# Gate and up of a feed-forward block made in parts of 512, 512 and 384 columns instead of four of 352, with new orders in the second pass

## What is computed

```
xn = layernorm(x)
Q, K, V = elu(xn@Wq+bq)+1, elu(xn@Wk+bk)+1, xn@Wv+bv          # 16 heads of 64
KV = einsum('bshd,bhdm->bhdm', K, V);  Z = 1/(Q . sum(K) + eps)
a  = einsum('bshd,bhdm,bsh->bshm', Q, KV, Z) @ Wo + bo
x1 = layernorm(xn + a)*g1 + be1
s  = layernorm(x1 + gelu(x1@W1+b1)@W2 + b2)*g2 + be2
xq = fp4(xn)                                                   # blocks of 16, also the weights
h  = silu(xq @ wg.T) * (xq @ wu.T)                             # 704 wide
g  = silu(fp4(h) @ wd.T)
out = x + s*g
```

## Time and profile before

| what | value |
|---|---|
| median of 3 runs | 1630.44 us (1628.6 to 1631.35) |
| the profiled execution | 1627.72 us |
| its span (first to last instruction) | 1625.9 us |
| PE busy | 1598.0 us, 98% |
| DVE busy | 1277.0 us, 79% |
| ACT busy | 977.1 us, 60% |
| POOL busy | 788.5 us, 48% |
| DMA | 123.96 MB, 76 GB/s on average |
| granted TensorE clock | 0.999 over the span |

### The profile page before, as it was taken

The page is one execution under the profiler, slowest core; times in us unless marked ns, Lnnn a source line. Parts: engine busy times, 40 slices in busy tenths (PEclk is TensorE's granted clock), DMA queues, the critical chain, the costliest instruction groups (busy, mean ns, idle before and its releaser), DMA issues.

```text
span 1625.9 us, 30464 instructions
## 1 busy us (share of the span) xinstructions
PE 1598.0 (98%) x10977; PEld 1439.4 (89%) x10977; DVE 1277.0 (79%) x2487; ACT 977.1 (60%) x1770; POOL 788.5 (48%) x750
## 2 busy tenths in 40 slices
PE   8999999999999999999999999999999999999997
PEld 6878888888889998989999999989899999999897
DVE  6786665545688797978888887979788888879797
ACT  6665665656465747465665657474755656574743
POOL 4564544434242636455544546364555445463636
PEclk9999999999999999999999999999999999999999
DMA  7422322331511111122121112111111221111110
GB/s 226 137 88 85 107 68 102 106 116 65 168 36 55 53 54 53 55 108 59 68 86 55 53 54 107 55 53 54 53 58 65 100 99 54 55 53 55 53 54 27
DMA packets 90531, 123.96 MB, mean 76 GB/s; under 512 B 10496, under 2 KB 58764, under 8 KB 89359
## 3 DMA queue, kind: packets, MB, share of 16 engines
q1 hardware_dynamic: 90382, 122.03, 23.0%
HBM read 86.86 MB, written 35.14 MB: 75 GB/s over the span
## 4 chain that ended last, share of the span: by engine, by line
PE 83%; DVE 9%; issue 3%; ACT 3%; POOL 2%; DMA 0%; DVEq 0%; SPq 0%; POOLq 0%; ACTq 0%
PE QH L81 11%; PE QH L82 11%; PE QH L83 11%; PE AC L81 7%; PE AC L83 7%; PE AC L82 7%; PE GU L81 5%; PE GU L83 5%; PE GU L82 5%; PE TT L834 2%; PE DN L726 2%; PE DN L81 2%; PE DN L82 2%; PE DN L83 2%; DVE rl L1846 1%
## 5 line engine op out<-in xcount | busy, mean ns | idle before, releaser
L2321 POOL TENSOR_TENSOR hb<-hb,rs_h 128x704 f32<-128x704 f32 x64 | 89.1, 1392 | 206.3 <-DVE rs_h L1689 206.3
L1253 ACT ACTIVATE hb<-GU 128x352 f32<-128x352 f32 x128 | 59.2, 463 | 214.7 <-PE GU L83 214.7
L1206 ACT ACTIVATE rh<-QH 128x512 fp32r<-128x512 f32 x256 | 150.4, 599 | 39.0 <-DVE QH L1837 35.4
L81 PE MATMUL GU<-wgh,xqh 128*128 128x352 f32 x512 | 169.5, 331 | 2.9 <-DVE hb L1682 2.9
L83 PE MATMUL GU<-wgh,xql 128*128 128x352 f32 x512 | 165.1, 322 | 0.0
L82 PE MATMUL GU<-wgl,xqh 128*128 128x352 f32 x512 | 164.9, 322 | 0.0
L2327 POOL TENSOR_TENSOR hb<-hb,sn_h 128x64 f32<-128x64 f32 x64 | 18.8, 293 | 296.9 <-DVE hb L1694 296.9
L1852 DVE TENSOR_TENSOR rl<-QH,rh 128x512 fp32r<-128x512 f32 x128 | 86.0, 682 | 85.6 <-ACT rh L1206 83.5
L81 PE MATMUL AC<-w2h,rh 128*128 128x256 f32 x512 | 145.8, 285 | 0.0
L81 PE MATMUL AC<-Mh,rh 128*128 128x256 f32 x512 | 145.3, 284 | 0.1
L82 PE MATMUL AC<-w2l,rh 128*128 128x256 f32 x512 | 142.4, 278 | 0.0
(11 more groups left out here) (235 smaller groups left out, 5589.3 us busy)
## 6 DMA issues: line engine op xcount, KB each, us to landing
zb<-z_scratch SPq DMA_DIRECT2D x128, 256.0 KB, 3.5
xa<-in_L_attn_src SPq DMA_DIRECT2D x16, 512.0 KB, 4.2
xt_scratch<-xth SPq DMA_DIRECT2D x32, 256.0 KB, 2.6
xt_scratch<-xtl SPq DMA_DIRECT2D x32, 256.0 KB, 3.0
xb<-in_L_attn_src SPq DMA_DIRECT2D x16, 512.0 KB, 4.0
xnTh<-xt_scratch SPq DMA_DIRECT2D x32, 256.0 KB, 4.8
xnTl<-xt_scratch SPq DMA_DIRECT2D x32, 256.0 KB, 5.5
out<-x SPq DMA_DIRECT2D x15, 512.0 KB, 6.6
```

What stands on the lines that cost most here:

```text
L81: e.matmul(outp, lh, rh, start=start, stop=False, skip_group_check=check)
L1206: e.activation(RH[j % 4][:], src, ACT.Copy).then_inc(S[sem], 1)
L1253: e.activation(HB[i % 3][:, hf * HALF:(hf + 1) * HALF], gu_bank(i, hf)[:, 0:HALF], ACT.Tanh, scale=0.5).then_inc(S["th"], 1)
L2321: e.tensor_tensor(hb, hb, spread(rs_h[i % 2][:], 44), ALU.mult).then_inc(S["hin"], 1)
```

## The change

The weights lie in other sections: 512 gate, 512 up, 192 gate, 192 up. `gate_up(i, 0)` makes 512 gate columns into the first bank and 512 up columns into the second, with a signal after each; `gate_up(i, 1)` makes 192 gate and 192 up in one product of 384 columns in one bank, the first for even tiles and the second for odd, with one signal. A tile has 12 matmuls of 512 and 6 of 384 columns. The waits are for the part that is overwritten alone: `hu` where only the gate columns of the bank must have been read, `hh` where up columns. `gate_tanh` and `gate_mul` work on 512 and 192 columns. The code that loads the weights follows the sections, and a few unused columns of SBUF are put between tensors. The bank choice "QH" for gate_up, unused before, is gone. Lines shift by one to some eighty (mm3 is L80 to L82 then).

```diff
-HALF = 352
+HEAD = 512
+SECTIONS = ((0, 512, 0, 0), (512, 512, 1, 0), (1024, 192, 0, 512), (1216, 192, 1, 512))
-GU_ORDER = (((0, 1), "GU"), ((0, 0), "GU"), ((1, 0), "GU"), ((1, 1), "GU"), ((2, 1), "GU"), ((2, 0), "GU"), ((3, 0), "GU"), ((3, 1), "GU"))
+GU_ORDER = ((0, 0), (0, 1), (1, 1), (1, 0), (2, 0), (2, 1), (3, 1), (3, 0))
+GU_ENDS = [sum(2 - hf for _, hf in GU_ORDER[:n + 1]) for n in range(8)]
...
             def gate_up(i, hf):
...
-                    tile, half = v[k - 1]
-                    w.wait_ge(S["hh"], hh_done(4 * (g if k else g - 1) + tile, half) if g or k else 0)
-                for part in range(2):
-                    c = hf * 704 + part * HALF
-                    for kt in range(2):
-                        last = mm3(e, bank[:, part * 512:part * 512 + HALF], xqh[:, kt, o:o + 128], xql[:, kt, o:o + 128],
-                                   wgh[:, kt, c:c + HALF], wgl[:, kt, c:c + HALF], kt == 0, kt == 1)
-                last.then_inc(gu_done(i, hf)[0], 1)
+                n = 8 * g + GU_ORDER.index((t, hf))
+                if hf:
+
+                    w.wait_ge(S["hu" if t % 2 == 0 else "hh"], n if t % 2 == 0 else n - 1)
+                    for kt in range(2):
+                        last = mm3(e, GU[:, t % 2 * 512:t % 2 * 512 + 384], xqh[:, kt, o:o + 128], xql[:, kt, o:o + 128],
+                                   wgh[:, kt, 1024:1408], wgl[:, kt, 1024:1408], kt == 0, kt == 1)
+                    last.then_inc(S["guG"], 1)
                 else:
 
+                    for up in range(2):
+                        if t % 2:
+                            w.wait_ge(S["hh"], n - 1 + up)
+                        else:
+                            w.wait_ge(S["hh" if up else "hu"], n)
+                        c = up * 512
+                        for kt in range(2):
+                            last = mm3(e, GU[:, c:c + 512], xqh[:, kt, o:o + 128], xql[:, kt, o:o + 128],
+                                       wgh[:, kt, c:c + 512], wgl[:, kt, c:c + 512], kt == 0, kt == 1)
+                        last.then_inc(S["guG"], 1)
...
+                e.scalar_tensor_tensor(hb, hb, 1.0, gate, ALU.add, ALU.mult).then_inc(S["hu"], 1)
                 w.wait_ge(S["hu"], n)
-                e.tensor_tensor(hb, hb, bank[:, 512:512 + HALF], ALU.mult).then_inc(S["hh"], 1)
+                w.wait_ge(*gu_done(i, hf, 1))
+                e.tensor_tensor(hb, hb, up_cols(i, hf), ALU.mult).then_inc(S["hh"], 1)
```

More of the change, by code:

```diff
@@ L96, in gate_up_rows @@
         while at < t * 128 + 128:
-            s, r = at // HALF, at % HALF
-            n = min(t * 128 + 128 - at, HALF - r)
-            row = (s // 2) * HALF + r
+            start, size, up, row = [x for x in SECTIONS if x[0] <= at < x[0] + x[1]][0]
+            n = min(t * 128 + 128 - at, start + size - at)
+            row += at - start
             last = rows[-1] if rows else None
-            if n == 128 and last and last[3] == 128 and last[4] == s % 2 and last[5] + 128 * last[1] == row:
+            if n == 128 and last and last[3] == 128 and last[4] == up and last[5] + 128 * last[1] == row:
                 rows[-1] = (last[0], last[1] + 1) + last[2:]
             else:
-                rows.append((t, 1, at % 128, n, s % 2, row))
+                rows.append((t, 1, at % 128, n, up, row))
             at += n
@@ L933, in _ @@
             turn_h(0, 1)
+            gate_up(2, 1)
             turn_x1(0, 0)
             turn_x1(0, 1)
-            gate_up(3, 0)
+            gate_up(3, 1)
+            down(0)
             h_proj(0, 0)
             h_proj(0, 1)
-            down(0)
-            f_step(0, 0)
+            gate_up(3, 0)
             h_proj(0, 2)
             h_proj(0, 3)
+            f_step(0, 0)
             f_step(0, 1)
@@ new lines, in _ @@
+            gelu(0, 4)
+            x_norm(1, 3)
+            gelu_hi(0, 4)
+            gelu(0, 5)
+            gelu_hi(0, 5)
+            h_abs(2)
+            gelu(0, 6)
+            gelu_hi(0, 6)
+            h_hi(1, 0)
+            gelu(0, 7)
+            gelu_hi(0, 7)
+            h_hi(1, 1)
+            q_exp(1, 0)
+            q_exp(1, 1)
+            h_hi(2, 0)
+            q_exp(1, 2)
+            q_exp(1, 3)
+            x_abs(1, 0)
+            h_abs(3)
+            g_tanh(1)
+            h_hi(2, 1)
@@ L1451, in _ @@
+            q_exp(1, 4)
+            q_exp(1, 5)
+            q_exp(1, 6)
+            q_exp(1, 7)
+            xq_hi(1, 0)
+            x_abs(1, 1)
+            for g in range(1, NG - 1):
+                a, b, c, d = 4 * g, 4 * g + 1, 4 * g + 2, 4 * g + 3
+                gate_tanh(a, 0)
+                gate_tanh(a, 1)
+                gate_tanh(b, 1)
+                ln_norm("lnb", g - 1, 0)
                 h_hi(d - 4, 0)
@@ new lines, in _ @@
+                xq_hi(g + 1, 0)
+                x_abs(g + 1, 1)
+            gate_tanh(NT - 4, 0)
+            gate_tanh(NT - 4, 1)
+            gate_tanh(NT - 3, 1)
+            h_hi(NT - 5, 0)
+            z_hi(NG - 1, 0)
+            z_hi(NG - 1, 1)
+            z_hi(NG - 1, 2)
+            g_tanh(NT - 6)
+            gate_tanh(NT - 3, 0)
+            z_hi(NG - 1, 3)
+            h_hi(NT - 5, 1)
+            ln_norm("lnb", NG - 2, 0)
+            z_hi(NG - 1, 4)
+            z_hi(NG - 1, 5)
@@ new lines, in _ @@
+            h_abs(NT - 4)
+            ln_norm("lnb", NG - 2, 1)
+            ln_norm("lnb", NG - 2, 2)
+            z_hi(NG - 1, 6)
+            z_hi(NG - 1, 7)
+            xq_hi(NG - 1, 1)
+            ln_norm("lnb", NG - 2, 3)
+            h_hi(NT - 4, 0)
+            gate_tanh(NT - 2, 0)
+            g_tanh(NT - 5)
+            h_hi(NT - 4, 1)
+            ln1_norm(NG - 1, 0)
+            ln1_norm(NG - 1, 1)
+            x1_hi(NG - 1, 0)
+            x1_hi(NG - 1, 1)
+            gate_tanh(NT - 2, 1)
@@ L2208, in _ @@
             z_mul(NG - 1, 5)
[L2209 removed]
+            h_lo(NT - 5, 1)
             z_lo(NG - 1, 4)
```

573 lines of the change are left out of this document (286 added, 287 removed).

## The result

The changed kernel took 1642.47 us (median of 4 runs, 1640.38 to 1645.65) against 1630.52 for the kernel before (4 runs): ratio 1.0079, 95% interval 1.0064 to 1.0095, so **12 us slower**. The forecast was 1623.6, with 1614 to 1634 as its range; the time lies outside, on the side to which I had given 0.13.

A forecast was written before the change was run, and what follows sets the result against it. TensorE, busy 98% of the span, was taken to bound the kernel, by its matmuls and once-a-period waits. -4.0 - 5.1 + 5.3 - 3.0 = -6.8 us, from the median 1630.44 to 1623.6 us; range 1614 to 1634.

The forecast's parts named there:

- The z stretch: den_inverse, two DMAs, z_mul, z_hi and z_lo ahead of at_step 0: covered by 0.5 us, so cost nothing.
- Rival 2: DVE sets the pace in the z stretch, with x_round, ln_add or statistics late: 1637.1 us; chance 0.12.
- Term A: Gate_up on PE: fewer matmuls per tile, 12 of 512 and 6 of 384 columns instead of 24 of 352; -4.0 us.
- Term B: PE's wait of den_sums on the last q_elu, 0.34 us a period, goes: -5.1 us.
- Term C: New wait of gate_up(a,1) on hu right behind gate_up(a,0), taken as 0.35 us a period: +5.3 us.
- theory 3: Set up after the measurement: the new round trips on hu in gate_up are the loss.
- The second wait on hu: gate_up(c,1) after gate_up(c,0), with turn_h(a,1) between: covered by 0.14 us, so cost nothing.
- Ends: First group -0.5 us, last group's end -1.8, two waits of the last group's turns -0.7: -3.0 us together.

The follow-up runs named there:

- late_h_in: The changed kernel with one more wait on GpSimd: h_in(a) starts only when z_mul 5 of its group is done; 1627.67 us, ratio 0.9991.
- parts_alone: The kernel before with its old orders on all engines and only the new gate and up parts, with coarse waits (hh); 1639.25 us, ratio 1.0061.
- gelu_first: late_h_in with gelu_hi 7 ahead of x_norm(g+1,1) on ScalarE and gelu_lo 7 ahead of h_round(c) on VectorE; 1669.06 us, ratio 1.0239.
- turn_between: late_h_in with turn_h(d-4,0) moved between gate_up(a,0) and gate_up(a,1) on TensorE; 1628.12 us, ratio 0.9987.
- all_mended: late_h_in plus the edits of turn_between and gelu_first, and gate_up(0,0) ahead of den_sums(0) in the first group; 1670.02 us, ratio 1.0246.
- turn_start: all_mended without the swaps of gelu_first; 1628.09 us, ratio 0.9986.
- before_pool_shifted: The kernel before with one unneeded GpSimd product of 512 elements more per group, started when z_mul 5 is done; 1631.08 us, ratio 1.0007.
- down_between: The changed kernel with down(c-4) moved between gate_up(a,0) and gate_up(a,1) on TensorE; 1660.61 us, ratio 1.0193.
- turn_start_hi: turn_start with gelu_hi 7 ahead of x_norm(g+1,1) on ScalarE alone; 1627.35 us, ratio 0.9983.
- before_pool_op: The kernel before with one unneeded GpSimd product of 512 elements more per group, started when z_lo 3 is done; 1645.09 us, ratio 1.0096.
- h_scale_late: The changed kernel with h_scale(a) moved behind z_mul 5 in VectorE's order, nothing added; 1628.20 us, ratio 0.9985.
- parts_fine: parts_alone with waits as fine as in the changed kernel (hu where only the gate's bank is overwritten); 1638.95 us, ratio 1.0054.

## Why the prediction was wrong, step by step

**The z stretch: the step that failed.** "DVE's work and ACT's stay what they were (products of 512 and 192 in place of 352 twice). Cost nothing". I worked out at_step 0, and rightly: PE reaches it 0.75 us (median) after z_lo 0, where I had said 0.5. But for "later steps are 0.1 to 0.3 us apart from theirs" I looked at no row, and the change puts h_scale(a) into that part of DVE's order, with POOL's h_in(a) started by it beside z_mul 5. At_step 4 had 0.15 to 0.2 us of cover at best, and got 0.8 of h_scale and 1.2 of collision ahead of it. late_h_in prices the collision at 14.3 to 14.8 us, 14.4 by the periods. The 0.8 us of h_scale(a) itself is covered: in late_h_in it stands at the same place, and at_step 4 starts 0.41 us (median) after its z_lo, 0.26 over the least.

**Rival 2** was right in its place (DVE sets the pace in the z stretch) and wrong in its mechanism: not x_round, ln_add or statistics late, but one z_mul held by POOL. That its time, 1637.1, lies nearest the measured one of all the rivals is partly luck, since it was worked out for a lateness at at_step 0, which did not come. Its chance of 0.12 was too small, and "DVE has 21% idle" was no argument against it: an order that is waited for at several places in 10 us has no use for idle time elsewhere.

**Term A, -4.0.** The rates are nearly right: rows of the kernel after around the gate_ups,

```profile
1117.84 0.39 PE L82 MATMUL GU<-wgh,xql 128*128 128x512 f32 x1
1118.25 0.44 PE L80 MATMUL GU<-wgh,xqh 128*128 128x384 f32 x1
1118.54 0.34 PE L81 MATMUL GU<-wgl,xqh 128*128 128x384 f32 x1
1118.71 0.34 PE L82 MATMUL GU<-wgh,xql 128*128 128x384 f32 x1
```

a 384 every 0.17 us (forecast 0.1736). The mean of all such distances without a wait is 0.1755 for 384 and 0.2296 for 512 columns: 48 x 0.2296 + 24 x 0.1755 against 96 x 0.1599 is 0.12 us a period saved, 1.9 us in all, half of the term. The term hangs on 2 ns a matmul, less than the pitch changes by itself (last section). What was missing: the same parts are longer products on DVE, and under the old orders they cost 9 us (parts_alone). A term of PE has a counterpart on the engine that reads its result.

**Term B, -5.1.** The wait of 0.34 went, but 0.10 is left at the new place (from the last f_step to den_sums 0.21 us where 0.11 is due): 0.24 x 15 = -3.6.

**Term C, +5.3.** From 1117.84 to 1118.25 are 0.41 and on to 1118.54 0.29, where 0.228 and 0.173 were due: 0.30 a period, forecast 0.35. The mechanism and nearly the size were right, and theory 3 with it falls: the gate_up part as a whole is even (-0.12 by A, -0.34 by the wait that stood at its end, +0.30 by C, and 0.17 more in gaps of about 0.1 us behind the first matmul of a step, five instead of three, which the trace puts down to no wait). Whether covering this wait would win its 0.3 us back was not shown: both attempts to cover it made another.

**The second wait on hu:** none, as said.

**Not foreseen:** q_proj 1 waits for gelu_hi 7 and gelu_lo 7, 0.23 us a period, 3.2 us in all. On DVE h_round(c) stood ahead of gelu_lo 7 before too; what is new is that down(b) no longer lies between q_proj 0 and 1 on PE, so that q_proj 1 comes 2 us sooner. The other way, a wait inside turn_x1 is gone: its eight transposes take 0.71 us a period instead of 1.10, 5.4 us in all, for which no term stood. And at the start at_step 6 of group 0 waits. h_round(0) now stands ahead of z_lo 6 and 7 on DVE, as in the other groups, but there PE has a down ahead of at_step 5, and here none:

```profile
452.66 0.28 PE L82 MATMUL AC<-Mh,rl 128*128 128x256 f32 x1
454.91 0.36 PE L80 MATMUL AC<-Mh,rh 128*128 128x256 f32 x1 [1.97 <-DVE rl L1928]
```

**Ends, -3.0.** Measured -1.3 at the end: 1.0 of it behind PE's last matmul (5.1 us to DVE's last row instead of 6.1, forecast 4.3). The first group is 1.7 longer instead of 0.5 shorter, with the wait above and the fall of the clock behind it. So the term came out at +0.4.

So of the 18.8 us between the forecast (-6.8) and the result (+12), the collision is 14.3 to 14.8. The 4 or so left are the ends and the first group (3.4), q_proj 1 (3.2), A (2.1) and B (1.5), less turn_x1 (5.4) and C (0.8). These come to 4.0; that they fit so well is partly luck, since gaps and pitches of a few tenths a period moved between the steps besides.

## What to carry to other kernels

When an order of one engine changes, list what each moved instruction starts on the other engines, and lay that beside what runs there; here a step of 0.8 us moved by a few lines woke a GpSimd instruction at the worst moment. Read the distance between release and start for every step of the tightest chain, not for the first alone: the step with 0.2 us of cover decides. And a narrow wait is only worth removing when what moves back has more cover than the wait is long (gelu_first paid 2.0 us, and the clock on top, for 0.25).

## What the runs showed of the hardware

**VectorE and GpSimd hold each other up.** A z_mul that meets a running GpSimd product of 704 columns takes 1.88 us instead of 0.69 and ends 0.55 us after it, as if it started only when that is nearly done. A TENSOR_SCALAR of 44 elements, 0.17 us alone, took 1.36 (the row at 1187.42 above) and ended 0.04 us after POOL's instruction. Products with one operand in PSUM took their usual 0.68 beside it, and instructions that read a single SBUF tile, as a TENSOR_REDUCE of 704 (0.88) or a RECIPROCAL of 128 (0.95), were not held either. It goes both ways: h_in took 1.75 instead of 1.39 when z_mul 4 had begun just before it. The Trainium skill (SBUF — State Buffer, SBUF: two separate sides) says that the two engines share a port pair under an exclusive lock for the whole instruction, and that a VectorE instruction with two SBUF inputs takes part in it against a GpSimd one that reads SBUF. The traces agree on who is held, with these numbers; I had not weighed that rule. The TENSOR_SCALAR has one SBUF input and so is not covered by that sentence; no run here shows why it is held. And for the whole instruction the traces do not agree. In the kernel before, POOL's ln_rstd of 4 columns, which reads and writes SBUF, runs beside z_mul 0 and 1 of group 5 (812.58 in the earlier trace rows):

```profile
812.60 1.54 POOL L2367 TENSOR_TENSOR rsblnb<-vtlnb,nhalf 128x4 f32<-128x4 f32 x1
```

It takes 1.54 us, 1.02 where no z_mul has begun just ahead of it, and both z_muls keep 0.69, the second though it starts within it. In group 2 a z_mul starts 0.10 us behind it and keeps 0.69 too. So this GpSimd instruction did not hold VectorE; whether that is for its few columns or for its operation (a power), no run shows.

The collision is common and mostly free: h_round's first half averages 1.22 us instead of 0.89 in the kernel after and in late_h_in alike, without a wait of PE on it. The group of late_h_in:

```profile
L1776 DVE SCALAR_TENSOR_TENSOR hb<-hc,hb 128x704 f32<-128x704 f32 x57 | 69.4, 1218 | 7.5 <-ACT hc L1276 7.5
```

**The clock can fall after a short idle.** In group 0 of the kernel after, PE was idle for 2.0 us ahead of 454.91 (the row above), worked at full rate for 0.8, and then had half the clock, 1.2 GHz, from 455.69 to 459.10, 3.4 us:

```profile
455.70:458.90 3.20, 3.20 (x18) 0.50 0.02 6
```

A matmul of 256 columns then starts every 0.21 us instead of 0.117. gelu_first shows the same in 11 of its 14 periods and not in the other three, with idles of the same length, and turn_between has no fall behind the idle of 1.9 us at this place. So such a wait of 2 us cost PE about 1.5 us more than its own length where the clock fell, and it did not fall each time.

In the first pass the clock falls in some executions and not in others: from 46 to 53 us in after, late_h_in, parts_alone, gelu_first, all_mended and turn_start, for 3.4 us in before_pool_shifted, down_between, turn_between and turn_start_hi, and not in before, before_pool_op, h_scale_late and parts_fine. The first of these rows is of before_pool_shifted, which has the old parts, the second of h_scale_late, which has the new ones:

```profile
47.70:51.00 3.30, 3.30 (x9) 0.50 0.02 5
```

```profile
46.10:52.90 6.80, 6.80 (x35) 1.00 0.01 2
```

So it goes with neither the parts nor the orders. PE wasn't idle ahead of it, it costs up to 2.7 us, and its cause stays open.

**A pitch that changes.** In at_step the matmuls of 256 columns start every 0.117 us (median) in the kernel after and in late_h_in, every 0.114 in the kernel before and in parts_alone. By the means (0.1145 and 0.1166 in at_step, 0.1153 and 0.1164 in f_step) that is 0.3 us a period, as much as each of the terms that I argued over. All five kernels with the old orders have 0.114, two of them with the new parts, so it doesn't go with the parts; turn_between and turn_start, with new orders and one turn elsewhere, have 0.114 in at_step again. No run here shows the cause.
